# Queries and keys projected token-major, rotated there and turned by TensorE, with new banks and a new order of the layer steps

## What is computed

```python
Q = rotate((ln(X) @ Wq), cos, sin); K = rotate((ln(X) @ Wk), cos, -sin); V = ln(X) @ Wv
att = einsum('bnhd,bmhd->bhnm', Q, K) * Dm        # Dm: decay by head, lower triangle
Y = groupnorm(einsum('bhnm,bmhd->bnhd', att, V)) * gn_s + gn_b
X = X + (swish(ln(X) @ Wg) * Y) @ Wo
X = X + gelu(ln(X) @ W1) @ W2
```

## Time and profile before

| | us |
|---|---|
| median of 3 runs | 781.1 (779.81 to 781.23) |
| the profiled execution | 781.24 |
| its span, first to last instruction | 779.4 |
| TensorE busy, share of the span | 658.2, 84% |
| DVE busy | 622.9, 80% |
| ACT busy | 417.2, 54% |
| POOL busy | 429.1, 55% |

### The profile page before, as it was taken

The page is one execution under the profiler, slowest core; times in us unless marked ns, Lnnn a source line. Parts: engine busy times, 40 slices in busy tenths (PEclk is TensorE's granted clock), DMA queues, the critical chain, the costliest instruction groups (busy, mean ns, idle before and its releaser), DMA issues. The chain is left out here.

```text
span 779.4 us, 13077 instructions
## 1 busy us (share of the span) xinstructions
PE 658.2 (84%) x4791; PEld 430.8 (55%) x4800; DVE 622.9 (80%) x1519; ACT 417.2 (54%) x729; POOL 429.1 (55%) x380
## 2 busy tenths in 40 slices
PE   4997798898988833748899999999999999899994
PEld 1444444444444332634667667777666666667773
DVE  6479798999989686467688888888888888779886
ACT  1996786776767305444454444444444444355551
POOL 6113587696887848464665555555555555551222
PEclk9997799999999986789999999999999999999997
DMA  9003132332344100000000000000000000000001
GB/s 324 7 5 54 35 100 89 86 96 81 84 100 85 55 2 0 0 1 1 2 1 22 1 6 15 22 2 4 15 2 21 2 7 13 1 1 1 1 25 32
DMA packets 17297, 27.36 MB, mean 35 GB/s; under 512 B 2320, under 2 KB 7056, under 8 KB 16976
## 3 DMA queue, kind: packets, MB, share of 16 engines
q1 hardware_dynamic: 17232, 26.51, 12.8%
HBM read 25.32 MB, written 1.18 MB: 34 GB/s over the span
## 5 line engine op out<-in xcount | busy, mean ns | idle before, releaser
L573 POOL TENSOR_TENSOR arena<-arena 128x1024 f32<-128x1024 f32 x64 | 150.0, 2359 | 52.3 <-PE psum L1322 27.3
L991 DVE TENSOR_TENSOR_SCAN arena<-arena,psum 128x1024 f32<-128x1024 f32 x64 | 141.8, 2267 | 3.3 <-issue 2.0
L1322 PE MATMUL psum<-arena,Cs 128*128 128x512 f32 x256 | 121.9, 599 | 1.2 <-POOL arena L573 1.2
L510 POOL TENSOR_TENSOR ve<-mv,eps 128x4 f32<-128x4 f32 x52 | 16.0, 307 | 191.7 <-DVE mv L889 191.7
L705 ACT ACTIVATE arena<-arena 128x510 f32<-128x510 f32 x128 | 84.8, 711 | 51.8 <-DVE arena L991 49.8
L620 POOL TENSOR_TENSOR arena<-arena,mhalf 128x32 f32<-128x32 f32 x16 | 86.8, 5428 | 2.3 <-DVE arena L1108 2.3
L1214 PE MATMUL psum<-Cs,arena 128*128 128x128 f32 x240 | 39.6, 290 | 42.9 <-ACT arena L748 25.9
L1407 PE MATMUL psum<-arena,Wl 128*128 128x512 f32 x128 | 67.4, 639 | 8.6 <-DVE arena L1092 5.3
L1322 PEld LDWEIGHTS psum<-arena,Cs 128*128 128x128 f32 x256 | 45.2, 191 | 46.3 <-issue 35.0
L1214 PEld LDWEIGHTS psum<-Cs,arena 128*128 128x128 f32 x240 | 28.6, 147 | 62.6 <-issue 28.3
L1305 PE MATMUL psum<-Cs,arena 128*128 128x128 f32 x256 | 35.2, 284 | 23.9 <-ACT arena L727 20.7
(11 more groups left out here) (172 smaller groups left out, 1415.6 us busy)
## 6 DMA issues: line engine op xcount, KB each, us to landing
arena<-c_rows_by_state SPq DMA_DIRECT2D x32, 512.0 KB, 4.8
Wl<-wl SPq DMA_DIRECT2D x4, 384.0 KB, 3.2
Wd<-wd SPq DMA_DIRECT2D x1, 1100.0 KB, 10.8
X<-x SPq DMA_DIRECT2D x4, 256.0 KB, 6.4
Sel<-sel SPq DMA_DIRECT2D x1, 1024.0 KB, 8.3
Wl<-wl SPq DMA_DIRECT2D x4, 256.0 KB, 3.0
out<-X SPq DMA_DIRECT2D x4, 256.0 KB, 2.3
Cs<-const SPq DMA_DIRECT2D x1, 614.0 KB, 9.2
```

The costliest lines, as they stand in the source:

```text
L573: pool.tensor_tensor(Hc[:, h], Hs[:, r, h], Crows[:, r], ALU.mult).then_inc(hc_ready, 1)
L991: dve.tensor_tensor_scan(Hs[:, turn % 2, h], Da[:, h], rows_of(turn, h), 0.0, ALU.mult, ALU.add).then_inc(scanned, 1)
L1322: ins = pe.matmul(bank[h], ident, Hc[:, h, group(e)], start=False, stop=False, skip_group_check=True)
```

## The change

Queries and keys are now projected token-major: the normalised rows are the stationary operand, tile by tile, and the 256 unswapped columns of both weights move past them, into two banks of two tiles each. DVE multiplies each bank once with a table of cosines and once with one of sines, into `Tc` and `Ts`. POOL adds each feature's cosine product to its neighbour's sine product, the even and the odd features in instructions of their own. TensorE turns the sums, keys and queries in a bank each (a new part in `spread`), and ACT spreads from those banks and also copies the turned queries to `Qr`. The mixed rows of all groups use bank 6, which leaves bank 7 to keys, states, ffn_up and ffn_down; the experts' results use banks 6 and 7 under the same claims. The times in `SCHEDULE`, and so the order, are new: TensorE's order in a window becomes gate, ffn_up, heads, spread 0, spread 1, ffn_down, out_turn, scores 0, keys, out, values, scores 1, turn1, states, rotate, ffn_turn, mix; DVE's becomes gate, heads, ffn_down, stats1, scale, scores 0, norm1, out, stats2, var, scores 1, norm2, states, rotate, unit.

```diff
-                   ("tq", 2 * S), ("tk", 2 * S), ("rank", EXPERTS))
+                   ("turn_cos", 4 * D), ("turn_sin", 4 * D), ("rank", EXPERTS))
...
 SCHEDULE = (
...
+    (0.192, "stats1", 0), (0.399, "norm1", 0), (0.533, "turn1", 0), (0.816, "rotate", 0), (1.087, "spread", 0),
+    (1.142, "spread", 1), (1.309, "keys", 0), (1.296, "scores", 0), (1.515, "values", 0), (1.012, "gate", 0),
+    (1.516, "scores", 1), (1.562, "states", 0), (1.957, "mix", 0), (2.010, "gather", 0), (2.068, "heads", 0),
+    (2.295, "square", 0), (2.509, "var", 0), (2.835, "unit", 0), (3.161, "out_turn", 0), (3.276, "scale", 0),
+    (3.447, "out", 0), (3.507, "stats2", 0), (3.532, "norm2", 0), (3.912, "ffn_turn", 0), (4.053, "ffn_up", 0),
+    (4.152, "ffn_down", 0),)
...
-            "rotate": ((1, rotated, 1), (4, rotated, 2), (5, rotated, 3), (1, rotated, 4)),
-            "values": ((4, v_ready, 1),), "gate": ((1, sg_ready, 1),),
-            "keys": ((4, k_tokens, 1), (1, k_tokens, 2)), "states": ((4, states, 1), (5, states, 2)),
-            "out": ((5, r_mid, 1),), "ffn_up": ((1, gelu_ready, 1), (4, gelu_ready, 2)), "ffn_down": ((5, r_newer, 1),)}
+            "rotate": ((4, rotated, 2), (1, rotated, 4)), "spread": ((5, k_spread, 1), (4, q_spread, 1)),
+            "values": ((1, v_ready, 1),), "gate": ((1, sg_ready, 1),),
+            "keys": ((7, k_tokens, 1), (5, k_tokens, 2)), "states": ((5, states, 1), (7, states, 2)),
+            "mix": ((6, yt_rows, 1),), "out": ((4, r_mid, 1),), "ffn_up": ((4, gelu_ready, 1), (7, gelu_ready, 2)), "ffn_down": ((7, r_newer, 1),)}
...
                     if what == "spread":
-                        dst, halves = ((Kr, Tk), (Qr, Tq))[part]
-                        pool.wait_ge(*added.at(layer, g - 2))
-                        pool.wait_ge(*rotated.at(layer, g, 2 * part + 2))
-                        pool.tensor_tensor(dst[:, half], halves[:, 0, half], halves[:, 1, half], ALU.add).then_inc(summed.sem, 1)
+                        pool.wait_ge(*rotated.at(layer, g))
+                        pairs = "p t (i e) -> p t i e"
+                        tiles = slice(g % 2 * GT, (g % 2 + 1) * GT)
+                        to, other = (v[:, tiles, part, :].rearrange(pairs, e=2) for v in (Tc, Ts))
+                        for e in range(2):
+                            ins = pool.tensor_tensor(to[:, :, :, e], to[:, :, :, e], other[:, :, :, 1 - e], ALU.add)
...
-                        act.wait_ge(*summed.at(layer, g, part + 1))
-                        count = (PARITY, 2)[part]
-                        for i in range(count):
+                        act.wait_ge(*kq_turned.at(layer, g, part + 1))
+                        act.wait_ge(*added.at(layer, g - 2))
+                        rows = bank[FILLS[what][part][0]]
+                        for i in range(2):
                             ins = act.activation(copies[:, chunks, i * CHUNK:(i + 1) * CHUNK],
-                                                 rows[:, half].rearrange("p (c n) -> p c n", n=CHUNK),
+                                                 rows.rearrange("p (c n) -> p c n", n=CHUNK),
                                                  ACT.Identity, scale=Cs[:, CS[masks]][:, i:i + 1])
...
+                        if part == 1:
+                            ins = act.copy(Qr[:, half], rows)
                         ins.then_inc(done.sem, 1)
...
                     if what == "rotate":
-                        for k in range(4):
-                            dve.wait_ge(*proj.at(layer, g, k + 1))
...
+                        dve.wait_ge(*kq_turned.at(layer, g - 2))
+                        for b in range(2):
+                            dve.wait_ge(*proj.at(layer, g, b + 1))
+                            tiles = slice(g % 2 * GT + 2 * b, g % 2 * GT + 2 * b + 2)
+                            for dst, table in ((Tc, "turn_cos"), (Ts, "turn_sin")):
+                                dve.tensor_tensor(dst[:, tiles].rearrange("p t a d -> p (t a d)"), bank[FILLS[what][b][0]],
+                                                  Cs[:, CS[table]], ALU.mult).then_inc(rotated.sem, 1)
...
-                        for k in range(4):
-                            pe.matmul(claim(what, k, layer, g), Wl[:, WL["qk"]][:, tile(k)], Ht[:, group(g)], start=True,
-                                      stop=True).then_inc(proj.sem, 1)
+                        kq = Wl[:, WL["qk"]].rearrange("p (a r d) -> p a r d", a=2, r=2)[:, :, 0, :]
+                        for b in range(2):
+                            dst = claim(what, b, layer, g)
+                            for t in range(2):
+                                ins = pe.matmul(dst[:, t * 2 * D:(t + 1) * 2 * D].rearrange("p (a d) -> p a d", a=2),
+                                                Ht[:, group(g)][:, tile(2 * b + t)], kq, start=True, stop=True)
+                            ins.then_inc(proj.sem, 1)
+                    if what == "spread":
+                        pe.wait_ge(*summed.at(layer, g, part + 1))
+                        dst = claim(what, part, layer, g)
+                        for t in range(GT):
+                            ins = pe.transpose(dst[:, tile(t)], Tc[:, g % 2 * GT + t, part, :], ident)
+                        ins.then_inc(kq_turned.sem, 1)
...
-                        pe.wait_ge(*yt_rows.at(layer, g - 2))
+                        rows_y = claim(what, 0, layer, g)
                         for b in range(2):
-                            y = bank[6 + g % 2][:, b * S:(b + 1) * S]
+                            y = rows_y[:, b * S:(b + 1) * S]
...
                 if what == "expert":
-                    n = RESULTS.index((g, part))
-                    dst = bank[6 + n % 2]
...
+                    b = 6 + RESULTS.index((g, part)) % 2
+                    dst = bank[b]
+                    for event, of, at_group, nth in held.get(b, ()):
+                        pe.wait_ge(*event.at(of, at_group, nth))
+                    held[b] = [(Results(mixed), one, g, part + 1)]
```

More of the change, by code:

```diff
@@ L94, in constants @@
     decay = np.log(decay.astype(np.float32)).astype(np.float64)
[L95 to L98, removed]
+    cosines, sines = np.zeros((P, 2, 2, D)), np.zeros((P, 2, 2, D))
+    for f in range(D):
+        h, i = divmod(f, DH)
+        grow = np.exp(pos.astype(np.float64) * decay[h])
         cos, sin = np.cos(ang[:, i // 2]), np.sin(ang[:, i // 2]) * (-1 if i % 2 == 0 else 1)
[L100 to L103, removed]
+        for a, (here, there) in enumerate(((cos / grow, -sin / grow), (cos * grow, sin * grow))):
+            cosines[:, :, a, f] = here.reshape(2, P).T
+            sines[:, :, a, f ^ 1] = there.reshape(2, P).T
+    c[:, CS["turn_cos"]] = cosines.reshape(P, -1)
+    c[:, CS["turn_sin"]] = sines.reshape(P, -1)
     c[:, CS["rank"]] = np.arange(EXPERTS, 0, -1)
@@ L157, in at, with __init__ @@
         return self.sem, count
-SCHEDULE = (
[L164 to L169, removed]
+class Results:
+    def __init__(self, sems):
+        self.sems = sems
+    def at(self, layer, g, k):
+        return self.sems[g], k
+SCHEDULE = (
+    (0.192, "stats1", 0), (0.399, "norm1", 0), (0.533, "turn1", 0), (0.816, "rotate", 0), (1.087, "spread", 0),
[4 more added lines that the diff above has]
+    (4.152, "ffn_down", 0),)
 def layer_order():
@@ L401, in four_blocks @@
         w1_done, gelu_ready, w2_done = per_group("w1_done", 2), per_group("gelu_ready", 2, 1), per_group("w2_done")
-        primed = (hn_rows, rotated, summed, v_ready, sg_ready, k_tokens, masked, states, added, yt_rows, centred,
+        primed = (hn_rows, kq_turned, v_ready, sg_ready, k_tokens, masked, states, added, yt_rows, centred,
                   gy_affine, r_mid, f_rows, gelu_ready)
@@ L610, in layer_steps @@
                     if what == "spread":
[L612 to L615 removed]
+                        pool.wait_ge(*rotated.at(layer, g))
[4 more added lines that the diff above has]
+                            ins = pool.tensor_tensor(to[:, :, :, e], to[:, :, :, e], other[:, :, :, 1 - e], ALU.add)
+                            if e == 0:
+                                own.put(ins)
+                        ins.then_inc(summed.sem, 1)
                     if what == "var":
@@ L816, in layer_steps @@
                         act.wait_ge(*added.at(layer, g))
-                        act.copy(Yt[:, half], bank[6 + g % 2]).then_inc(yt_rows.sem, 1)
+                        act.copy(Yt[:, half], bank[FILLS["mix"][0][0]]).then_inc(yt_rows.sem, 1)
                     if what == "square":
```

26 lines of the change are left out of this document (8 added, 18 removed).

## The result

| | before | after |
|---|---|---|
| median of 6 runs each | 781.16 us | 775.88 us (774.55 to 778.85) |
| ratio, 95% interval | | 0.9931 (0.9907 to 0.9955) |
| span of the profiled execution | 779.4 us | 773.7 us |

The kernel became faster, by 5.3 us or 0.7%. The forecast was 17 us: the time lies inside the range of 757 to 778, but less than a third of the gain arrived. Lines have moved: L1128 is now L1146, L1067 L1085, L1092 L1110, L900 L919, POOL's sums L628 and its power for `var` L636, rotate L1428, spread L1435 with ACT's copies L822 and L828, scores L1464, heads L1499, gate L1447, gather L836, `unit` L1131, `scale` L1135, transposes L1232, ffn_up L1517, and L1239 serves ffn_down and other products.

The account below looks back on a forecast made before the run. A closed loop of 20.80 us windows, DVE late then TensorE, was taken as the bound. Thirteen windows at -1.3 (-16.9), opening +0.8 and norm2 -0.9 gave -17.0 from 781.1: 764 us, range 757 to 778.

Parts of the forecast that it names:

- Loop, sign and mechanism: Repeating window: DVE late for 9.32 us, then TensorE for 11.48; rotate stops waiting for state masks, window 20.80 to 19.5 us.
- The 2.0 us by which TensorE's work was to fall: TensorE, each window: rotate from 4.63 to 1.73 us, two spread steps adding 0.88, so 2.0 us less work.
- POOL's sum, 0.72 us: POOL's four 256-element stepped sums: 0.72 us each, from a line through three trace rows; spread 1 waits 0.2 us.
- ACT: ACT's spread copies from a bank and the added plain query copy: 0.66 us each, hidden with 0.4 us to spare.
- Gate's wait for the last rotation product: TensorE's gate claims bank 1, held by DVE's second rotation pair, so it starts at T+13.32, T being the add's start.
- Edges: Outside the repeating rhythm: one more loop window, opening plus 0.8, norm2 after the last add minus 0.9, ending nothing net.
- the 13th window's -1.3: One more loop of the same kind before the first add at 412.99, also 1.3 us shorter.
- nothing for the next two, which POOL sets: Opening: the first group's chain grows by 0.8 us, the next two groups by nothing; bounds 0 and 3.
- Nothing net: Ending, bank 7: two 1.06 us waits go, two of about 0.45 come in each of two groups; bounds minus 2, plus 10.
- the ending takes it back: Rival: three claims on bank 7 in each of three tail groups cost 9.5 us, about 774 us; chance 0.12.
- The 0.9 of norm2: After the last add, TensorE's 2.93 us stand for norm2 shrinks by 0.9 because norm2 precedes the state masks.
- sums at 0.98 us: Halfway case of the rival that POOL's sums are dear: window 20.5 us, time about 777 us; chance 0.06.

Follow-up runs that it names:

- the run of all three: Changed kernel with bank 5 for ffn_up's second product and ffn_down in the ending, extra opening transposes, and POOL's sums on runs of 8: 764.21 us, ratio 0.9774.

## Why the prediction was right and wrong

- **Loop, sign and mechanism: right.** The forecast that 9.32 us of DVE and 11.48 us of TensorE make one loop, and that rotate would leave the DVE part, held: 19.79 against 19.5, and 19.38 without POOL's wait, where the same sum without that wait gives 19.3. One bank instead of two costs 4.1 us a window, 1.3 of them by the clock, norm2 behind states 0.38, and 1.73 us of the projection's work put back costs 0.71. So each of the three parts of the change matters to the window; how the 1.01 us divides among them does not show, since each edit trades one stand for another. The 2.0 us by which TensorE's work was to fall counts waiting as work: eight products of 512 columns take 3.54 us without a wait (in the kernel before, 365.67 to 369.21), so the work falls by some 0.9. The sum does not use this number.
- **POOL's sum, 0.72 us: mis-sized.** It measured 0.846, and 3.71 for four in the window where I had 3.35. That covers the whole difference of the loop: 0.29 us in each of 12 windows, 3.4 us of what is missing. The row that I called nearest in kind was not: in L437 one input and the output have the step of two and the other input is contiguous, and in L435, named beside it as reading and writing every second element, only the output has it. Those rows rise by 2.0 ns an element (0.209 us for 8, 0.322 for 64), as contiguous ones do; the new sums, with the step in both inputs and the output, cost 2.5 (0.846 less 0.207, over 252 elements). Runs of 8 measured 0.722, what the line gave. The Trainium skill, GPSIMD Engine Reference, section "Performance pitfalls for Q7 kernels", puts the surcharge at steps over 8 bytes. Here a step of 8 bytes in both inputs and the output costs 17% over runs of 8 (0.846 against 0.722), so the trace agrees neither with no surcharge nor with a half.
- **ACT: right.** 0.605 each where I took 0.66, and covered. Where POOL's wait is gone, the scores stand 0.4 us for the last of them, and `out` no longer stands for DVE, so that it stays covered.
- **Gate's wait for the last rotation product: not in the loop.** DVE's rotate ends at 468.79 and mix holds TensorE until 469.05. It is there in the opening only, 1.38 us.
- **Failed: the step "Edges".** I gave the opening +0.8 besides the 13th window's -1.3 and the ending -0.9, and measured +3.1 and +3.4. Together these make 7.9 us, and loop and edges 11.3, all that is missing between the spans (5.7 instead of 17.0); the medians differ by 5.3.
  - *Opening.* The working counted two transposes and a copy on the chain, at the times of the steady window, and gave no thought to TensorE's clock. The runs show products at 1.2 GHz there, and that holding the clock takes the first two intervals from 36.27 us to 33.33, where 33.12 was the time before. Why the clock is late is not shown. That the shorter rotate, with new stands behind it, leaves it low is argued from one trace before and one after: rotate twice as long (5.42 us) did have gate at 1.12 behind it, but so had the short rotate in two other runs. My "nothing for the next two, which POOL sets" failed for the second interval (+1.2); in the third POOL does set the time once the clock is up, through rx_norm and gather, and with that order changed the sums and the clock do. 0.55 us of the +3.1 lie ahead of the first turn1, less than the executions differ there.
  - *Ending.* "Nothing net" for bank 7 was the wrong sum. The two waits of 1.06 us for ffn_up's bank did go; but I priced the new ones at 0.45 each and they were 1.12, 0.52 and 1.57, because DVE's sums of the experts come late, as the rival "the ending takes it back" said; it had 9.5 us for it, and 3.2 came. The 0.9 of norm2 was won where I put it (the stand at the first turn is 2.00 us) and partly given back: the turn after ffn_up then stands 1.04 us for its norm. Beyond bank 7 the third interval of the ending stays 0.85 us longer than before; its cause I did not follow.
- **The range held by luck.** Its upper part came from two cases, sums at 0.98 us and an ending of 9.5 us. Neither came; three smaller misses, in the loop, the opening and the ending, added up to about as much.

## What to carry to other kernels

A closed loop read from one window gives a good price for what repeats; an opening and an ending need a working of their own, wait by wait, with the clock that TensorE will have there and with what sits in each bank at that point. Where work is taken from TensorE ahead of a wait, ask whether what follows still runs at 2.4 GHz; 52 products that nobody reads took 2.9 us off two windows of the opening, and the third gave 1.9 of them back until its own stands were dealt with. And before a row is taken as the nearest in kind, count how many of its operands have the access pattern in question.

## What the runs showed of the hardware that I had not expected

- POOL's addition of 256 elements with a step of two floats in both inputs and the output takes 0.846 us, over runs of 8 neighbouring floats 0.722, in the same number of elements and instructions.
- DVE's `unit`, 512 elements with both inputs in SBUF, takes 0.68 us where it starts ahead of POOL's next instruction (385.90 in the run of all three; that instruction, a power, then takes 1.47 us instead of 1.01), 1.75 behind the start of a sum of 512 elements on POOL, 1.32 behind that of a sum of 256 with a step and 1.20 behind that of one on runs of 8: the shorter the POOL instruction that it meets, the sooner it ends. The Trainium skill, SBUF — State Buffer, section "Who interferes with whom", says that a VectorE instruction with two SBUF inputs contends with a GpSimd instruction that reads SBUF, and calls the pair of ports that they share an exclusive lock; the order of the durations agrees with that.
- A stand of some 3 us in every window (one bank for rotate) puts part of each window at 1.2 GHz even in the steady part: a granted clock of 0.50 from 512 to 514, and 1.59 us for six products of mix against 0.95.
